# Products of the input with the first weight, made on TensorE during the eigenvalue count and reloaded from DRAM

## The reference

```python
# layer 0: spectral filter; U holds the eigenvectors of the normalised Laplacian
agg = einsum('mn,bnd->bmd', U.T, x)
h   = relu(agg @ W1 + b1)
x   = layernorm(x + einsum('nm,bmd->bnd', U, h @ W2 + b2))
# layer 1: two graph convolutions, then for p = 1..4 an LSTM over windows of p nodes
# layer 2: graph attention, one head (W, a);  layer 3: masked attention, four heads (Wqkv)
```

## The kernel before, in words

| stage | PE | then |
|---|---|---|
| aggregate | L994: four 128-column products of x with U | ACT L1143 copies them (printed as L1127) |
| hidden | L997: one 512-column product with W1 | ACT L1146: relu with b1 |
| filtered | L1000: four products with W2 | DVE L1238: adds b2 |
| back | L1003: one 512-column product with UT | DVE L1242: adds x |
| norm_0 to norm_3 | | DVE L1248 to L1258, then POOL L962, L964 |
| apply_0 to apply_3 | | ACT L1138, four instructions |
| mix | L1007: four products with the adjacency | ACT copies (L1149, printed as L1127) |
| heads_turned | L1117: four transposes | DVE L1342, L1347 |

## Time and profile before

### The profile page before, as it was taken

One profiled execution on the slowest core, in us unless ns is written; L12 is line 12 of the kernel. 1 busy time (PEld: TensorE's weight loads), 2 busy tenths in 40 slices (PEclk: granted clock), 3 DMA queues, 4 the chain that ended last, 5 costly groups with the idle time before them and its releaser, 6 DMA issues.

```text
span 1481.8 us, 24437 instructions
## 1 busy us (share of the span) xinstructions
PE 1024.0 (69%) x6001; PEld 834.4 (56%) x6001; DVE 1125.8 (76%) x5634; ACT 793.1 (54%) x2905; POOL 172.3 (12%) x464
## 2 busy tenths in 40 slices
PE   5777777777640000008998889988799978899875
PEld 4666666666430000005796666976668956679754
DVE  6888888888799889983457784566865678845677
ACT  3555555555320000004777866777767778677786
POOL 2111111111200000001011010111020120201111
PEclk9999999999975555558999899999899999999987
DMA  0000000000200000001000010000010000100000
GB/s 2 1 1 1 1 1 1 1 1 1 56 20 1 1 1 1 1 0 57 1 2 1 1 39 22 1 1 1 8 53 1 1 1 2 30 0 1 1 1 29
DMA packets 19903, 12.94 MB, mean 9 GB/s; under 512 B 1153, under 2 KB 18722, under 8 KB 19746
## 3 DMA queue, kind: packets, MB, share of 16 engines
q1 hardware_dynamic: 19746, 11.23, 2.8%
HBM read 7.03 MB, written 4.19 MB: 8 GB/s over the span
## 4 chain that ended last, share of the span: by engine, by line
PE 32%; DVE 11%; ACT 8%; issue 2%; POOL 1%; DMA 0%; DVEq 0%; POOLq 0%; ACTq 0%
PE P L1036 11%; PE P L981 6%; PE P L1044 6%; ACT x L1138 2%; PE P L986 2%; ACT S L1209 2%; DVE stats L1248 2%; PE P L1098 1%; DVE S L1320 1%; DVE top L1325 1%; DVE t L1338 1%; PE P L1053 1%; PE P L1082 1%; POOL t L969 1%; ACT t L1189 1%
## 5 line engine op out<-in xcount | busy, mean ns | idle before, releaser
L461 PE MATMUL sumP<-ident_tail,Yb 128*128 128x128 f32 x1 | 0.5, 473 | 215.6 <-DVE Yb L623 215.6
L193 PE MATMUL productP<-M,ident_tail 128*128 128x127 f32 (+63 forms) x254 | 87.3, 441 | 71.3 <-DVE M L313 71.3
L1036 PE MATMUL P<-t,WihT 128*128 128x128 f32 (+1 forms) x832 | 119.4, 290 | 10.9 <-POOL t L969 10.9
L1044 PE MATMUL P<-step_h,WhhT 128*128 128x128 f32 (+2 forms) x768 | 123.4, 304 | 0.0
L490 ACT ACTIVATE small<-small 128x1 f32<-128x1 f32 x1 | 0.2, 203 | 229.1 <-DVE small L596 229.1
L461 PEld LDWEIGHTS sumP<-ident_tail,Yb 128*128 128x128 f32 x1 | 0.2, 183 | 215.7 <-DVE Yb L623 215.7
L1036 PEld LDWEIGHTS P<-t,WihT 128*128 128x128 f32 x832 | 109.9, 191 | 14.4 <-POOL t L969 13.7
L193 PEld LDWEIGHTS productP<-M,ident_tail 128*128 128x128 f32 x254 | 63.6, 311 | 95.1 <-DVE M L313 95.1
L1161 ACT ACTIVATE gate_i<-P,half_bias 128x128 f32<-128x128 f32 (+3 forms) x160 | 69.1, 432 | 89.3 <-PE P L1044 65.3
L962 POOL TENSOR_TENSOR rstd<-variance,minus_half 128x4 f32<-128x4 f32 x64 | 64.5, 1007 | 442.4 <-DVE variance L1258 442.4
L1044 PEld LDWEIGHTS P<-step_h,WhhT 128*128 128x128 f32 x768 | 108.9, 191 | 4.5 <-DVE step_h L1291 0.7
(11 more groups left out here) (322 smaller groups left out, 3159.6 us busy)
## 6 DMA issues: line engine op xcount, KB each, us to landing
xin<-x SPq DMA_DIRECT2D x16, 256.0 KB, 2.8
out<-y SPq DMA_DIRECT2D x16, 256.0 KB, 2.3
W<-L_gnn_W SPq DMA_DIRECT2D x3, 64.0 KB
Wqkv<-L_gnn_W SPq DMA_DIRECT2D x1, 192.0 KB
Wg<-L_gnn_Wg SPq DMA_DIRECT2D x2, 64.0 KB
A<-adj SPq DMA_DIRECT2D x1, 64.0 KB, 2.0
b<-L_gnn_b SPq DMA_DIRECT2D x1, 64.0 KB
bg<-L_gnn_bg SPq DMA_DIRECT2D x1, 64.0 KB
```

The costliest lines, as they stand in the source:

```text
L193: pe.matmul(productP[:, remaining], tails, M[:, remaining], start=True, stop=True).then_inc(product_ready, 1)
L1036: last = pe.matmul(place, c["WihT"][:, p - 1, gate * H:(gate + 1) * H], sources(s, p, t), start=bank not in fresh, stop=not t, skip_group_ ...
L1044: last = pe.matmul(gate_place(s, p, t, gate), c["WhhT"][:, p - 1, gate * H:(gate + 1) * H], step_h[s][:, 0:G * windows(p)], start=False, s ...
```

## The change

A new function, `feature_products`, gives SP, PE and ACT work in part 2. For each of 16 groups of four graphs SP loads x, PE transposes it, ACT copies the transpose, PE multiplies it with W1, ACT copies the product, and SP writes it to a DRAM scratch tensor. There are two buffers of each kind. PE does this behind the product of L459, ACT behind the copies of the constants and ahead of L490, SP behind the loads of the constants. In part 3 the scratch is loaded beside x into a new tile `xw`, on the same semaphore; stage "aggregate" and its copy are gone, and "hidden" is now four products of `xw` with U. The list of stages is one shorter, and `HEAD_STAGES` is 3. Eight semaphores are added to part 2.

```diff
-HEAD_STAGES = 4
+HEAD_STAGES = 3
@@ spectral_vectors
+    transfer, multiply, keep_products = products
             load(sp)
+            transfer(sp)
...
             pe.matmul(outP[:, 0:1], a[:], ones[:, 0:1], start=True, stop=True).then_inc(passed_summed, 1)
+            multiply(pe)
             pe.wait_ge(y_ready, 1)
...
             keep(act)
+            keep_products(act)
             act.wait_ge(norm2_ready, 1)
@@ feature_products (new)
+    def transfer(sp):
+        for k in range(2):
+            sp.dma_start(x_here[k][:], x_groups[k]).then_inc(fetched[k], 16)
+        for k in range(groups):
+            sp.wait_ge(made_kept, k + 1)
+            sp.dma_start(product_groups[k], made[k % 2][:]).then_inc(returned[k % 2], 16)
+            if k + 2 < groups:
+                sp.wait_ge(across_ready, k + 1)
+                sp.dma_start(x_here[k % 2][:], x_groups[k + 2]).then_inc(fetched[k % 2], 16)
+        for j in range(2):
+            sp.wait_ge(returned[j], 16 * (groups // 2))
+    def multiply(pe):
+        for k in range(groups):
+            j = k % 2
+            pe.wait_ge(fetched[j], 16 * (k // 2 + 1))
+            if k:
+                pe.wait_ge(across_kept, k)
+            for b in range(G):
+                last = pe.transpose(acrossP[:, b * N:(b + 1) * N], x_here[j][:, b, :], ident)
+            last.then_inc(across_ready, 1)
+            pe.wait_ge(across_kept, k + 1)
+            if k:
+                pe.wait_ge(made_kept, k)
+            for b in range(G):
+                last = pe.matmul(madeP[:, b * H:(b + 1) * H], x_across[j][:, b, :], c["W1"][:], start=True, stop=True)
+            last.then_inc(made_ready, 1)
+    def keep(act):
+        for k in range(groups):
+            j = k % 2
+            act.wait_ge(across_ready, k + 1)
+            if k > 1:
+                act.wait_ge(made_ready, k - 1)
+            nc.scalar.activation(x_across[j][:].rearrange("h g n -> h (g n)"), acrossP[:], ACT.Copy).then_inc(across_kept, 1)
+            act.wait_ge(made_ready, k + 1)
+            if k > 1:
+                act.wait_ge(returned[j], 16 * (k // 2))
+            nc.scalar.activation(made[j][:].rearrange("n g h -> n (g h)"), madeP[:], ACT.Copy).then_inc(made_kept, 1)
@@ layers
-    stages = ["aggregate", "hidden", "filtered", ...
+    stages = ["hidden", "filtered", ...
                 sp.dma_start(xin[s][:], x4[0, s]).then_inc(x_in[s], 16)
+                sp.dma_start(xw[s][:], p4[0, s]).then_inc(x_in[s], 16)
...
                     sp.dma_start(xin[s][:], x4[bass.ds(following, 1), s].squeeze(0)).then_inc(x_in[s], 16)
+                    sp.dma_start(xw[s][:], p4[bass.ds(following, 1), s].squeeze(0)).then_inc(x_in[s], 16)
...
-                if name == "aggregate":
-                    pe.wait_ge(x_in[s], trip * 16 + 16)
+                if name == "hidden":
+                    pe.wait_ge(x_in[s], trip * 32 + 32)
                     on("banks_free", s, trip)
-                    each(P[s][0], lambda b: xin[s][:, b, :], lambda b: U[:]).then_inc(S_("agg_ready"), 1)
-                elif name == "hidden":
-                    on("agg_copied", s, trip)
-                    pe.matmul(P[s][1][:], c["W1"][:], t1[s][:], start=True, stop=True).then_inc(S_("hidden_ready"), 1)
+                    each(P[s][1], lambda b: xw[s][:, b, :], lambda b: U[:]).then_inc(S_("hidden_ready"), 1)
...
-                elif name == "aggregate":
-                    on("agg_ready", s, trip)
-                    copy(t1[s][:], P[s][0][:], "agg_copied", s)
```

More of the change, by code:

```diff
@@ L331, in reversed_columns, with spectral_vectors @@
     return bass.AP(ap.tensor, ap.offset + (n - 1) * step, [[p_step, p], [-step, n]])
-def spectral_vectors(nc, sb, psum, sem, ident, ones, E, D, reflectors, gains, borders, U, UT, constants):
+def spectral_vectors(nc, sb, psum, sem, ident, ones, E, D, reflectors, gains, borders, U, UT, constants, products):
     QT = sb("QT", [N, N])
@@ L769, in load_constants, with feature_products @@
     return load, turn, keep, mark
-def layers(nc, sb, psum, sem, c, ident, U, UT, x_dram, out_dram):
+def feature_products(nc, sb, psum, sem, c, ident, x_dram, products_dram):
+    groups = B // G
+    x_groups = x_dram.rearrange("(k g) n d -> k n g d", g=G)
+    product_groups = products_dram.rearrange("(k g) n d -> k n g d", g=G)
+    x_here = [sb(f"x_here_{j}", [N, G, H]) for j in range(2)]
+    x_across = [sb(f"x_across_{j}", [H, G, N]) for j in range(2)]
+    made = [sb(f"made_{j}", [N, G, H]) for j in range(2)]
+    acrossP = psum("acrossP", [N, 512])
+    madeP = psum("madeP", [N, 512])
+    fetched = [sem(f"fetched_{j}") for j in range(2)]
+    returned = [sem(f"returned_{j}") for j in range(2)]
+    across_ready = sem("across_ready")
+    across_kept = sem("across_kept")
+    made_ready = sem("made_ready")
+    made_kept = sem("made_kept")
+    def transfer(sp):
[35 more added lines that the diff above has]
+            nc.scalar.activation(made[j][:].rearrange("n g h -> n (g h)"), madeP[:], ACT.Copy).then_inc(made_kept, 1)
+    return transfer, multiply, keep
@@ L781, in layers @@
     xin = tiles("xin", [N, G, H])
+    xw = tiles("xw", [N, G, H])
     x = tiles("x", [N, G, H])
@@ L862, in grouped @@
         return tile[s][:].rearrange("n (g h) -> n g h", g=G)
-    stages = ["aggregate", "hidden", "filtered", "back", "norm_0", "apply_0", "mix", "conv0", "lin1", "conv1"]
+    stages = ["hidden", "filtered", "back", "norm_0", "apply_0", "mix", "conv0", "lin1", "conv1"]
     stages += [("gates", 1, 0), ("output", 1, 0), ("cell", 1, 0)]
@@ L1397, in program @@
                 constants = load_constants(nc, c, sb_of(part), psum_of(part), sem_of(part), d, A, ident, ones)
+                products = feature_products(nc, sb_of(part), psum_of(part), sem_of(part), c, ident, d["x"], products_dram)
                 spectral_vectors(nc, sb_of(part), psum_of(part), sem_of(part), ident, ones, E, D, reflectors, gains, borders,
-                                 U, UT, constants)
+                                 U, UT, constants, products)
                 clear_semaphores()
         with ExitStack() as part:
-            layers(nc, sb_of(part), psum_of(part), sem_of(part), c, ident, U, UT, d["x"], out)
+            layers(nc, sb_of(part), psum_of(part), sem_of(part), c, ident, U, UT, d["x"], products_dram, out)
 NAMES = ("x", "adj", "L0_gnn_W1", "L0_gnn_b1", "L0_gnn_W2", "L0_gnn_b2", "L1_gnn_Wg0", "L1_gnn_bg0", "L1_gnn_Wg1",
```

3 lines of the change are left out of this document (added).

## The result

The changed kernel took **1474.09 us** (median of 6 runs, 1472.98 to 1478.26), the kernel before 1482.65 us beside it on the same chip (6 runs, 1481.74 to 1484.41): a ratio of 0.9947, with a 95% interval of 0.9932 to 0.9963. That is 8.6 us faster. The forecast was 1476.3 with a range of 1472 to 1482. The profiled execution took 1473.89 us, with a span of 1472.2.

A forecast was written before the change was run, and what follows sets the result against it. DVE works alone in part 2; at part 3's crossings DVE, then PE, then ACT at loop-backs sets the pace. Terms -2.5 - 2 x 0.85 - 2.2 + 0.5 = -5.9 us gave a median of 1476.3 us, range 1472 to 1482.

The forecast's parts named there:

- The products at nothing: Part 2: making the products on PE and ACT fits inside idle time while DVE works alone, so it costs nothing.
- The 102 us: Part 2: sixteen groups of transposes, copy, products and copy at 6.4 us each, half of the 215.6 us covering them.
- Traffic does not show as a longer stand, so I add nothing: Part 2: DMA traffic beside a loop-back of the count does not lengthen DVE's stand there; 0, bounded by 0 and 1 us.
- Clearing: Between parts 2 and 3: POOL clears eight more semaphores, +0.5 us, with 0.7 and 1.7 us as costlier estimates.
- Start: Start of part 3: second tile delays first matmul 0.9 us, aggregate and copy go; first mix 2.5 us sooner.
- The loop-backs: Two crossings between trips in part 3: ACT's last work before the branch ends sooner, -0.85 us each, bounds 0 and -2.2.
- then come the same branch, table load and relu 3, 3.58 us from ACT's last end to relu 3: Loop-backs: after ACT's last work before the branch, the time to relu 3 stays 3.58 us, so only 0.85 us is gained.
- that rival: More than forecast: branch not tied to ACT's last end, 2.2 us gained at each of three crossings, 1473.6 us; chance 0.08.
- The exit: Crossing into the last trip, without branch or table load: mix comes 2.2 us sooner, bounds -1.4 and -2.45.
- PE is not what ends last there: Places in part 3 where aggregates go: the obvious 18.6 us sum is too large, since DVE, then briefly PE, then ACT paces.
- The rival of the clock: Crossings: less PE work lowers its clock; short dips leave 1481.4 us (within no change, 0.22), long dips 1486.5 (chance 0.10).
- Nothing for the rest: Rest of part 3: hidden as four products, one more load per tile and the last trip's end change nothing.

## Why the prediction was right, and where not

**The products at nothing: right, with an unsound reason for one of its parts.** The cover held by far (64.5 us of 215.6), and part 3 began at the low clock as forecast. The 102 us were too many by over a third, harmlessly, since only their being under 215 mattered. Of the 38 us, some 17 are the transposes, which had been priced like products on the strength of rows 3, where no transpose stands (2.08 for an average of 1.01), 4 the products, which ran at the full clock for part of the time, and 16 the copies and hand-overs, which overlapped (2.2 us a group for 1.2). But "Traffic does not show as a longer stand, so I add nothing" rested on rows 10, one of which had no traffic beside it and the other only the writes of y. The stand was 4.21 us, +1.13 at the end of part 2, outside the bound of 0 to 1, and over the 4 us that the text had named as a sign against itself. The Trainium skill, page "Runtime: NRT & Kernel Launch", section "Instruction fetch mechanics", says that a taken branch out of the held pages waits for a fetch by DMA; by that rule traffic can lengthen it. The trace agrees: the instruction packet started 1.0 and 0.7 us later in the two executions whose transfers filled 495 to 497, and at its usual time in the five whose transfers paused there.

**Clearing: right.** +0.57 for +0.5, in every kernel that has the eight more.

**Start: right.** -2.97 for -2.5. The wait for a second tile came as costed (+0.74 for +0.9). The clock rose sooner in this execution than in the kernel before, which by the estimate above is worth 0.6 us, so that the change's own part is near -2.4. In four others (one of them with the trips written out) the start was 18.06 to 19.44 us instead of 17.97, so one to one and a half microseconds of this term are open from one execution to the next.

**The loop-backs: the term that was mis-sized.** -2.05 and -1.80 for -0.85 each. The order of the work came out as written, the bias of slot 0 first, 874.52. The step that failed is "then come the same branch, table load and relu 3, 3.58 us from ACT's last end to relu 3". From ACT's last end (878.79 + 1.64 = 880.43) to relu 3 at 882.53 it was 2.10 us: with fewer stages ahead, the last group before the branch is a long one and the branch runs beside it. The 3.58 us also held 0.26 us of waiting for PE: PE and ACT ended nearly together before the change already, and PE stood 1.30 us at its own branch, which the step leaves out. In the changed kernel relu 3 came 0.56 us behind the end of PE's products for it (881.97), and PE had lost its aggregate. It was the bound that I had given as -2.2 "if the stand at the branch is not tied to ACT's last instruction", the case to which I gave a chance of 0.08. The measured 1474.1 lies nearer to that rival's 1473.6 than to the forecast of 1476.3, and the first crossing, 2.05 us shorter, is over the 2 us that the text had named as a second sign against itself. Four head stages and three in the kernel before show that both moves were needed (loop-backs of 18.1 with either one alone), the trips written out that 1.8 us of the branch remain, of which PE's stand alone accounts for about 1.0.

**The exit: right.** -2.29 for -2.2; it needs the missing stage and nothing else, since it is 14.23 with four head stages as well, and 16.53 with three in the kernel before.

**"PE is not what ends last there": too strong.** Of the 18.6 us of aggregates, 9.1 came back (2.97 + 2.05 + 1.80 + 2.29), and the same work given back to PE cost 10 to 12. Rows 8 were read rightly for 872 to 876, where DVE is busy for 3.80 of 4; but PE takes over behind DVE for longer than "a few microseconds".

**The rival of the clock did not come.** No stretch of the crossings left 1.00 with PE at 2.67 to 3.07 us in 4, although the aggregates were gone. "Nothing for the rest" was wrong in another way: -2.29 us lie in code that did not change. Of these, 1.68 are in the tail and go with 11 us less at the low clock; the changed kernel's other profiled execution had 3.2 us more there than the kernel before and took 1.60 us longer. So it is the execution's and no gain of the change. Without it the parts give -7.4 us, and some -6.8 without the sooner clock at the start; the means of all executions, 1475.4 for the changed kernel (12) and 1482.5 for the one before (63), differ by 7.1. The forecast of -5.9 was short by 1.5 us for that reason: 2.15 from the loop-backs and 0.56 from start and exit, less 1.2 for the count and the clearing. That the sum came out inside its range is in part luck: terms that were too small and a term put at nothing stand against each other in it.

**The signs.** PE idled 153.2 us before L464, for about 110. From the first matmul to the first mix it took 14.28 us, for 14.6, and from the first mix to that of trip 2 196.9, for 199.5: the loop-back's 1.2 us more, and 1.4 in the middle of the trip, which the change does not touch.

## What to carry to other kernels

Work that PE does for every tile can be made ahead under a stretch in which another engine works alone, and kept in DRAM; the price here was 0.07 us for each semaphore more and a load more per tile, and the gain is not the work that goes but what ends last at the places where it goes: here 9 of 18.6 us. Where a branch stands at such a place, look at the stand of every engine and not of one, count it from when its last instructions were queued and not from their end, and try the number of stages ahead of it anew with every change of the work: neither the shorter head nor the lighter PE gave anything at the loop-backs alone. And when a few microseconds matter, compare the stretches that a change doesn't touch first, for their clock can make a difference of microseconds by itself.

## What the runs showed that I had not expected

- A loop-back of the count stood for 4.21 and 3.84 us in two of seven executions with DMA traffic, 3.05 to 3.15 us in the eleven others. Each ended 1.9 to 2.0 us behind the start of one 8 KB packet of instructions, which came late in those two.
- PE stood at its own branch for 0.80 to 2.44 us, longest (2.44 and 2.01) with four products more per tile.
- Before ACT's table load at a loop-back, the stand counted from ACT's last end ran from 0.32 to 2.48 us; counted from the start of the last group queued it ran from 1.96 to 3.17. With the trips written out one table load of 1.28 us is left in part 3 instead of three, so the two at the loop-backs belong to the loop and not to the functions used.
- The same kernel falls into two bunches some 5 us apart; its two profiled executions, 1473.89 and 1479.24 us, differ mostly in where the low clock lies in stretches of equal code. Some 3.4 us more at the low level cost only about 1 us.
- Eight loads of 256 KB in place of four, issued in alternation, delayed the first matmul by 0.74 us only, and a second tile from scratch landed as soon as a second one from x (medians of 3.2 and 3.3 us from issue).
